# A two-layer transformer block on one core: query projection in pairs of groups, new routes for keys, powers and constants, filler matmuls, and a new table of steps

## The reference

```
x = x + xattn0(layernorm(x), ctx)      # l = 0
x = x + ffn0(layernorm(x))             # low-rank term of the top-1 of 8 experts
x = x + xattn1(layernorm(x), ctx)      # l = 1
x = x + moe1(layernorm(x))             # 8 experts, top 1

xattn: q = x@Wq.T+bq; k, v from ctx (77 rows); 16 heads of 8 features
       p = softmax((q@k.T * tau + delta) / sqrt(8)); out = (p@v)@Wo.T+bo
moe1:  t@switch_w+switch_b -> softmax -> route = argmax, prob = max
       out = (gelu(t@w1[route]+b1)@w2[route]+b2) * prob
```

## Time and profile before

| what | us |
|---|---|
| median of 3 runs | 214.88 (213.81 to 215.64) |
| the profiled execution: its own time | 216.53 |
| its span on the core | 214.7 |
| PE busy in the span | 177.7 (83%) |
| DVE / ACT / POOL busy | 133.5 / 90.5 / 62.3 |

### The profile page before, as it was taken

The page is one execution under the profiler, slowest core; times in us unless marked ns, Lnnn a source line. Parts: engine busy times, 40 slices in busy tenths (PEclk is TensorE's granted clock), DMA queues, the critical chain, the costliest instruction groups (busy, mean ns, idle before and its releaser), DMA issues.

```text
span 214.7 us, 3672 instructions
## 1 busy us (share of the span) xinstructions
PE 177.7 (83%) x1157; PEld 144.8 (67%) x1157; DVE 133.5 (62%) x385; ACT 90.5 (42%) x178; POOL 62.3 (29%) x68
## 2 busy tenths in 40 slices
PE   7658999999798987689978989983499749999960
PEld 2323797898684955376873769872388749999950
DVE  1899876596585359868351788455247356677750
ACT  2333146542554132531334244531354637777720
POOL 8690024000674020020006000025002734555461
PEclk9969699999999999999997999999558999999996
DMA  5899500000029300000000000002710281000000
GB/s 188 277 361 406 210 2 3 0 0 3 2 93 344 112 0 0 0 5 0 0 0 3 0 0 0 3 0 99 226 48 17 89 270 28 26 5 9 20 23 2
DMA packets 11983, 15.43 MB, mean 72 GB/s; under 512 B 1713, under 2 KB 8898, under 8 KB 11965
## 3 DMA queue, kind: packets, MB, share of 16 engines
q1 hardware_dynamic: 10444, 13.13, 18.4%
q0 software_dynamic: 1088, 1.60, 2.3%
q10 hardware_dynamic: 432, 0.47, 0.6%
...
## 4 chain that ended last, share of the span: by engine, by line
PE 54%; DVE 22%; issue 7%; ACT 5%; DMA 4%; another core or an unknown queue 2%; POOL 2%; DVEq 1%; ACTq 0%; POOLq 0%
PE acc L911 10%; PE scores L1012 7%; PE acc L1023 6%; PE shared L850 5%; PE scores L892 4%; PE shared L968 3%; PE shared L954 3%; DVE MR L658 3%; PE shared L867 3%; DVE QG L649 2%; PE shared L941 2%; DMA X<-in_x 2%; DVE XN L604 2%; PE shared L822 2%
## 5 line engine op out<-in xcount | busy, mean ns | idle before, releaser
L911 PE MATMUL acc<-VP,P 123*128 123x128 f32 (+1 forms) x320 | 41.8, 276 | 0.9 <-ACT P L535 0.9
L911 PEld LDWEIGHTS acc<-VP,P 123*128 123x128 f32 (+1 forms) x320 | 39.8, 191 | 3.5 <-ACT P L535 2.0
L535 ACT ACTIVATE P<-scores 123x512 f32<-123x512 f32 (+1 forms) x40 | 23.1, 595 | 30.8 <-PE scores L892 24.4
L461 POOL TENSOR_TENSOR X<-X,ROWS 128x512 f32<-128x512 f32 x6 | 8.1, 1352 | 76.5 <-DVE XN L604 76.4
L1012 PE MATMUL scores<-XST,HT 128*128 128x128 f32 x176 | 26.4, 298 | 4.5 <-ACT XST L565 3.5
L658 DVE TENSOR_REDUCE MR<-shared 128x4 f32<-128x308 f32 x64 | 27.3, 472 | 2.5 <-PE shared L867 2.2
L1012 PEld LDWEIGHTS scores<-XST,HT 128*128 128x128 f32 x176 | 23.7, 210 | 6.2 <-ACT XST L565 4.7
L475 POOL DMA_INDIRECT out<-XS,token x22 | 21.4, 974 | 19.6 <-DVE XS L790 16.8
L1023 PE MATMUL acc<-W,HT 128*128 x176 | 23.2, 276 | 0.2 <-DVE XS L790 0.2
L850 PE MATMUL shared<-XNT,ATT 128*96 128x512 f32 x32 | 19.0, 710 | 4.9 <-DVE VP L644 3.1
L867 PE MATMUL shared<-KG,QG 98*128 98x308 f32 x64 | 21.0, 375 | 2.1 <-DVE QG L649 1.4
...
## 6 DMA issues: line engine op xcount, KB each, us to landing
...
```

Of the source, the lines that this page charges most:

```text
L535: act.activation(P[0:w, n % NP], scores[n % 2][0:w, :], ACT.Exp).then_inc(probs_ready, 1)
L911: ins = pe.matmul(acc[qt // 2][:, c:c + VW], P[0:w, n % NP, 128 * qt:128 * qt + 128], VP[0:w, l, b, j, half], start=(t == 0 and qt % 2 == ...
```

## The change

The same computation, with these edits:

- **q**: one matmul of 128 output rows makes two groups (`pair`); ACT and DVE still handle each group by itself. A group's queries are read from 64 rows of PSUM (before 96), and the remainder's rows from the other copy.
- **keys**: ACT writes `Ks` rounded at once, per batch; DVE makes the remainder in one operation per batch. `Kt` is gone. `km` waits for its own batch.
- **first arrays**: `small` (delta, tau, selectors; 128 x 159) is the first DMA of ACT's queue; delta's and tau's own DMAs are gone. tau is scaled by DVE. The ones of `QG` are set by DVE ahead of all else; POOL fills `VP` before it waits for an input.
- **powers**: in the last stage the reciprocal root and the exponential of the routing are `pow` on POOL, not Ln/Exp on ACT. The one-hot is written as bf16 at once.
- **empty rows**: `slots` is filled from a constant DRAM array, issued by SP after its loads; the blanking on POOL is gone.
- **filler**: a step `warm` issues 4 matmuls on zeros into the bank of the next step that takes one.
- **table**: new. One `warm` behind the first `q` of layer 1, three behind the last `wo`; `moe/0` stands before `route/1`, `moe/1` before `rank/1`.

```
-        max/1/1/... wo/1/1 ln/3/1
-        moe/-1 xn/3/1 xt/3/1 route/1 prob/1 moe/0:2 rank/1 tiles/1
+        sc/1/1/7 rank/0 prob/0 sc/1/1/8 ... pv/1/1/8:10 on/1/1 tiles/0 ot/1/1 wo/1/1 ln/3/1
+        warm/16 warm/19:21 xn/3/1 moe/-1 xt/3/1 moe/0 route/1 moe/1 prob/1 rank/1 tiles/1
...
-            finish(pool.memset(QG[ONES:ONES + 2, 0].bitcast(F32), 1.0), zeroed)
...
+            finish(pool.memset(VP[:, :, :, :, :, HALF * VC:], 0.0), zeroed)
             pool.wait_ge(in_con, 16)
-            finish(pool.tensor_scalar(tau8[:, :], TAU[:, :], RS8, None, ALU.mult), tau_ready)
...
-                finish(pool.memset(XS[:, :, :], 0.0), blank)
-                finish(pool.tensor_copy(XS[:, :, R_ID], CON[:, C_SID:C_SID + NS]), blank)
...
+                if s[0] == "ln" and s[1] == 3:
+                    b = s[2]
+                    pool.wait_ge(var_ready, b + 1)
+                    pool.tensor_tensor(rstd[:, b], var_eps[:, b], mhalf[:, :], ALU.pow).then_inc(rstd3_ready, 1)
+                if s[0] == "route":
+                    b = s[1]
+                    pool.wait_ge(lg_ready, b + 1)
+                    pool.tensor_tensor(ex[:, b], euler[:, :, :], lg[:, b], ALU.pow).then_inc(ex_ready, 1)
...
-                        act.activation(Kt[:, :, b], Kf[:, :, b], ACT.Identity, scale=tau8[0:QR, b:b + 1]).then_inc(k_scaled, 1)
+                        act.activation(Ks[0:QR, :, b], Kf[:, :, b], ACT.Identity, scale=tau8[0:QR, b:b + 1]).then_inc(k_high, 1)
...
-                    act.activation(QG[0:QR, b, g], bank(s)[0:QR, :], ACT.Identity,
-                                   bias=ATT[l][0:QR, A_BQ + g:A_BQ + g + 1]).then_inc(qh_ready, 1)
+                    for odd in (0, 1):
+                        g, r = 2 * pair + odd, slice(64 * odd, 64 * odd + 64)
+                        act.activation(QG[0:64, b, g], bank(s)[r, :], ACT.Identity,
+                                       bias=ATT[l][r, A_BQ + g:A_BQ + g + 1]).then_inc(qh_ready, 1)
...
+            for b in range(B):
+                dve.memset(QG[ONES:ONES + 2, b].bitcast(F32), 1.0).then_inc(ones_row, 1)
...
+                        dve.tensor_scalar(var_eps[:, b], mean_var[:, b, :, 1], EPS, None, ALU.add).then_inc(var_ready, 1)
...
-                    link(dve.tensor_copy(Ks[0:QR], Kt[:, :, :, :]))
-                    dve.tensor_tensor(Ks[32:64], Kt[32:64], Ks[32:64].bitcast(F32), ALU.subtract).then_inc(k_split, 1)
+                    for b in range(B):
+                        dve.wait_ge(k_high, B * l + b + 1)
+                        dve.scalar_tensor_tensor(Ks[32:64, :, b], Kf[32:64, :, b], tau8[32:64, b:b + 1],
+                                                 Ks[32:64, :, b].bitcast(F32), ALU.mult, ALU.subtract).then_inc(k_split, 1)
...
+                if kind == "warm":
+                    key = next(k for k in map(first_key, steps[i + 1:]) if k in use)
+                    hold(key)
+                    for _ in range(BRIDGE):
+                        pe.matmul(bank(key)[:, :], idle[:, 0:128], idle[:, 0:S], start=True, stop=True)
...
-                    pe.matmul(bank(s)[0:QR, :], ATT[l][:, A_Q + QR * g:A_Q + QR * (g + 1)], XNT[:, b], start=True,
+                    pe.matmul(bank(s)[:, :], ATT[l][:, A_Q + D * pair:A_Q + D * (pair + 1)], XNT[:, b], start=True,
```

More of the change, by code:

```diff
@@ L122, in schedule @@
-        pv/1/1/1 sc/1/1/3 ln/3/0 mt/1/1/1 pv/1/1/2:4 sc/1/1/4:6 xn/3/0 xt/3/0 pv/1/1/4 sc/1/1/6 route/0 prob/0
-        pv/1/1/5 sc/1/1/7 pv/1/1/6 rank/0 sc/1/1/8 pv/1/1/7 sc/1/1/9 pv/1/1/8:10 on/1/1 ot/1/1 tiles/0 wo/1/1 ln/3/1
-        moe/-1 xn/3/1 xt/3/1 route/1 prob/1 moe/0:2 rank/1 tiles/1
+        ln/0/0 xn/0/0 vp/0/0/0 xt/0/0 delta q/0/0/0:2 kp/0 km/0/0 max/0/0/0:8 vp/0/0/1 max/0/0/8 vp/0/0/2 max/0/0/9
+        vp/0/0/3 max/0/0/10 mt/0/0/0 max/0/0/11 vp/0/0/4 sc/0/0/0:2 ln/0/1 max/0/0/12 vp/0/1/0 xn/0/1 max/0/0/13
@@ new lines, in schedule @@
+        xt/2/1 q/1/1/0:2 sc/1/0/8 pv/1/0/6 sc/1/0/9 max/1/1/0:3 pv/1/0/7 max/1/1/3 pv/1/0/8 max/1/1/4:9 pv/1/0/9
+        mt/1/1/0 on/1/0 sc/1/1/0 max/1/1/9 sc/1/1/1 max/1/1/10:13 sc/1/1/2 max/1/1/13:15 pv/1/1/0 max/1/1/15 ot/1/0
+        sc/1/1/3 mt/1/1/1 wo/1/0 sc/1/1/4 pv/1/1/1:4 ln/3/0 sc/1/1/5 pv/1/1/4 xn/3/0 xt/3/0 sc/1/1/6 pv/1/1/5 route/0
+        pv/1/1/6 sc/1/1/7 rank/0 prob/0 sc/1/1/8 pv/1/1/7 sc/1/1/9 pv/1/1/8:10 on/1/1 tiles/0 ot/1/1 wo/1/1 ln/3/1
+        warm/16 warm/19:21 xn/3/1 moe/-1 xt/3/1 moe/0 route/1 moe/1 prob/1 rank/1 tiles/1
@@ L169, in banks, with build @@
     return uses
-def build(nc, x, ctx3, att0, att1, consts, rows, delta, tau, ffn0w, loraB, sw, w1, b1, w2, b2, out):
+def build(nc, x, ctx3, att0, att1, consts, small, rows, ffn0w, loraB, sw, w1, b1, w2, b2, empty, out):
     steps = schedule()
@@ L545, in _ @@
                                        bias=W0[:, W_WIB + k:W_WIB + k + 1]).then_inc(hid_act, 1)
-                elif kind == "route":
-                    b = s[1]
-                    act.wait_ge(lg_ready, b + 1)
-                    act.activation(ex[:, b], lg[:, b], ACT.Exp).then_inc(ex_ready, 1)
                 elif kind == "moe":
@@ L1049, in constants @@
         c[:, C_TAIL + 4 * t + 1] = 128 * t + p
-    for t in range(NS):
-        c[:, C_SID + t] = B * S + 128 * t + p
     c[:, C_T:C_T + NSB] = np.arange(NSB)
@@ L1056, in constants, with small_rows, empty_slots @@
     return c
+def small_rows(delta, tau):
+    s = np.zeros((128, S_N), np.float32)
+    s[ONES:KR, S_DEL:S_DEL + B * KEYS] = delta.reshape(-1)
+    s[:, S_TAU:S_TAU + B] = tau
+    s[ONES, S_SEL] = 1
+    s[ONES + 1, S_SEL + 1] = 1
+    s[ONES + 2:KR, S_SEL + 2] = 1
+    return s
+def empty_slots():
+    rows = np.zeros((NS * 128, RW), np.float32)
+    rows[:, R_ID] = B * S + np.arange(NS * 128)
+    return rows
 def kernel(**inputs):
```

163 lines of the change are left out of this document (88 added, 75 removed).

## The result

The changed kernel is not faster. Forecast were 209.2 us and a gain of 5.7; measured is a loss of 1.3 us (0.0061 of 214.97). Some executions of either kernel take some per cent longer at a lower granted clock (one of the change, its first, took 291.4 us at 0.56): they are left out of the ratios and, from here on, of the medians, unless a median is said to be over all runs.

What follows compares the result with a forecast made beforehand. PE was taken to bound most (54% of the chain, DVE 22%), the experts' entry waits. Projections -3.0, second entry into layer 1 -1.0, start +0.3, experts' entry -2.0 make -5.7: 214.88 to 209.2 us, range 204.5 to 214.0.

Steps and rivals of the forecast that it cites:

- The entry into the mixture of experts: From the last `wo` to the tiles: filler, powers and new order shrink PE's idle; -2.0 us, ends -0.5 and -3.5.
- the prediction's own signs of being wrong: In the new profile: statistics late, DVE waiting for `ex`, or PE's gain turning up as waits for DVE in `max`.
- Rival 3: Routing and last normalisation: slow powers on POOL delay DVE; 5.7 us lost at P = 4.5, 222 us at P = 8; chance 0.10.
- P: Time of one 128 x 32 power on POOL, the routing's exponential; the forecast took 0.6 us.
- Projections: Query projections in both layers: 8 paired products issued instead of 16; -3.0 us, ends -2.2 and -4.1.
- Rest of the table: Other reorderings of steps, not priced row by row: 0, with 1 us either way.
- Second entry into layer 1: Layer 1, batch 1: a values product fills PE's 1.56 us wait and may keep the clock; -1.0 us, ends 0 and -2.3.
- Start: Kernel start: DVE's memsets delay statistics by 0.1 us, keys come behind queries on ACT; +0.3 us, ends -0.5 and +3.7.
- Rival 1: Start: DVE's and POOL's memsets take turns, statistics slip 1.3 to 3.7 us; 210.5 to 212.9 us, chance 0.17.
- W: The end of `wo/1/1`, 148.24 us in the kernel before; times at the experts' entry are counted from it.
- Free parts: Filler behind layer 1's first `q`, POOL's dropped blanking, the constant's copy, ACT's eight fewer small operations: said to cost or gain nothing.
- Rival 2: Layer 1: DVE, as busy as before, absorbs PE's savings; only layer 0's 1.7 and 0.7 remain; 212.5 us, chance 0.18.

Runs made afterwards that it cites:

- change_again: The change unedited, run once more beside the kernel before on one chip: median 214.99 us against 213.64, ratio 1.0068.
- between_again: The change with roots and both exponentials on ACT, no power on POOL, same order of steps: median 208.77 us, ratio 0.9726 to the kernel before.
- old_table_act: The change with the old order of steps, each query pair at its first member's place, no filler, no power on POOL: ratio 1.0108 to the kernel before.

## Why the prediction was wrong, step by step

**The step that failed** is the price of the power, in "The entry into the mixture of experts": "A power of 128 x 4 lies by size at the second, so 0.3, and 128 x 32 at 0.3 to 1.4; I take 0.6". Measured: 1.04 and 5.43 us. From that price came the walk's "exponential and rank till 12.9", with no wait of DVE for the exponential in it; DVE waited 3.28 and 4.39 us for the two, one of the prediction's own signs of being wrong. The ends of that estimate were rows of another kind (a scaling by a constant and an addition), and neither is a bound for a power. The estimate of 0.07 us plus the fixed part that the prediction took from the Trainium skill, "GPSIMD Engine Reference", section 3, rests on that page's rate for a two-input addition. The page prices no power, and against 5.43 us the rate is no guide to one.

**Rival 3** had the mechanism, the places and the size of it: P - 3.4 in batch 0, about P in batch 1. With P = 5.43 it gives 2.0 + 5.4, and the roots 0.6 (1.04 beyond a cover of 0.4): 8.0 us against a gain of 5.7, so +2.3. Measured is +1.3 to +1.5. By parts: all powers cost 6.2 us (medians of change_again and between_again) to 7.3 (their ratios). Of it batch 1's exponential is 3.1 to 3.4, where the rival had 5.4. The roots are 1.6 by the profiles, where it had 0.6. Batch 0's exponential is 1.8 to 2.2: from the statistics of batch 0 to those of batch 1 the change takes 19.75 and 20.21 us, the kernel without powers 17.18, with `wo/1/1` at half the clock in all three, and 0.8 of the difference is the root. PE's hole ahead of `ot/1/1` says the same, 3.39 us against 1.54. It had a chance of 0.10 because P was guessed; "at P = 4.5 it eats the whole gain" was right as far as can be told (at 5.43 the loss is 0.6 to 0.7%). The rule "P/8 for 128 x 4" was off too: if the time grows evenly with the elements, 1.04 and 5.43 make 0.41 us fixed and 0.157 us per element of a partition.

**All the rest together** was right in its sum: without powers the kernel has 0.9753 and 0.9726, that is -5.3 and -5.9 us against the forecast's -5.7. That is in part luck, since the terms were not what was forecast:
- Projections, forecast -3.0: at most 4.8 to 6.9 by doubling them in the new order, half of it or more lost at the start, where the forecast had no term; with the other edits in the old order no gain at all (+2.3 us for old_table_act). So the term is not confirmed, and it hangs on the table.
- Rest of the table, forecast 0: order and filler together bring 7.6 to 8.2 us to a kernel with pairs, where the two entries were to bring 3.0.
- Second entry into layer 1, -1.0: the hole shrank to 0.45 us and the clock held, as forecast. From 80 to 90 us the granted clock was 0.81 to 0.87 in eight of the 13 profiles with the new order and single pairs and 1.00 in five, where the kernel before has 1.00, so what the term gained in the end was not isolated.
- Start, +0.3: statistics at 5.53 against 5.3 forecast, DVE's memsets 1.76 us each against 1.94 at most. The run of maxima at 19.35 against 19.8. Rival 1 (0.17) is refuted: DVE's memset ran from 3.73 to 5.49 while POOL filled `VP` from 2.81 to 4.78. The Trainium skill, "SBUF — State Buffer", section "SBUF: two separate sides", lets a DVE operation in a 2-port performance mode or with two SBUF inputs contend for the shared ports. A memset has no input, and the trace shows no turns for this pair. The cast that had taken 1.97 us beside POOL's fill of `VP` takes 0.26 at 9.27, where that fill has been over since 4.78.
- Entry into the experts, -2.0: idle before the slots 0.77 (1.9 forecast), clock full behind the filler (half a chance), though it had dropped ahead of it; slots at W+4.3 (4.7 forecast). Without the powers the bias of tile 2 comes 13.1 us behind the sum of batch 1 (W+13.8 forecast), as this row of between_again and the one at 155.91 show:

```profile
142.79 0.69 DVE L703 TENSOR_TENSOR ROW<-X,shared 128x512 f32<-128x512 f32 x1 [3.00 <-PE shared L948]
```

- Free parts: the filler may be worth a little, some 1 us. Rival 2 (absorbed, 0.18) is out: 5.3 to 5.9 us are there once the powers are gone, where it had 2.4.

The range of 204.5 to 214.0 missed because it left out rival 3 altogether, though no row of the trace excluded its condition, P over 4.5.

Not settled: what stops PE, ACT and DVE for 2 to 6 us around the second reading of the slots on four of the five chips of the experiments. It is in the kernel before, too (DVE stands for 4.07 us from 169.3 in its profile), and it may decide how much of batch 1's power shows in the end.
